# ScalarE makes the masked step sizes of a Mamba-2 layer as 32 scaled 128x128 copies per pair, in place of four products on GpSimd

## What is computed

```
dt = jax.nn.softplus(dt + dt_bias)
A = -jnp.exp(A_log)
dA = jnp.exp(dt * A)

def step(h, inp):
    dA_t, dtx_t, B_t, C_t = inp
    h = h * dA_t[:, :, None, None] + dtx_t[..., None] * B_t[:, None, None, :]
    y = jnp.einsum('bhpn,bn->bhp', h, C_t)
    return (h, y)
```

## Time and profile before

| | us |
|---|---|
| median of three runs | 860.14 |
| lowest and highest of them | 856.6, 867.21 |
| span of the profiled execution, first to last instruction | 851.0 |

### The profile page before, as it was taken

One profiled execution on the slowest core, in us unless ns is written; L12 is line 12 of the kernel. 1 busy time (PEld: TensorE's weight loads), 2 busy tenths in 40 slices (PEclk: granted clock), 3 DMA queues, 4 the chain that ended last, 5 costly groups with the idle time before them and its releaser, 6 DMA issues. The chain is left out here.

```text
span 851.0 us, 13516 instructions
## 1 busy us (share of the span) xinstructions
PE 689.8 (81%) x3713; PEld 528.2 (62%) x3713; DVE 608.2 (71%) x1640; ACT 447.5 (53%) x967; POOL 543.4 (64%) x398
## 2 busy tenths in 40 slices
PE   3687897788788899979998999799993865577883
PEld 3255665567467677857786778567882744355662
DVE  2839969988987998999879987998673364122331
ACT  3665666565675677648755776376532321121230
POOL 1414333746547587867867788678678587537775
PEclk9798799798798999989989999899997798697997
DMA  5000001112114544554465345534755677757882
GB/s 185 12 1 0 1 26 38 50 51 63 44 49 123 137 117 95 135 129 111 95 162 117 91 112 113 145 69 112 175 132 126 169 174 163 169 130 149 202 180 26
DMA packets 81273, 88.85 MB, mean 104 GB/s; under 512 B 7360, under 2 KB 67696, under 8 KB 81200
## 3 DMA queue, kind: packets, MB, share of 16 engines
q1 hardware_dynamic: 54528, 61.37, 25.4%
q0 software_dynamic: 26672, 26.62, 17.4%
HBM read 54.50 MB, written 33.46 MB: 103 GB/s over the span
## 5 line engine op out<-in xcount | busy, mean ns | idle before, releaser
L466 POOL DMA_INDIRECT out<-xs x142 | 228.7, 1611 | 115.4 <-issue 53.3
L436 POOL DMA_INDIRECT rows<-payload,pos x128 | 133.3, 1041 | 46.4 <-issue 30.9
L884 DVE SCALAR_TENSOR_TENSOR xbc<-T,table,xbc 128x511 f32<-128x511 f32 (+2 forms) x192 | 141.7, 746 | 7.6 <-ACT xbc L616 3.0
L1459 PE MATMUL FX<-wt,hid 128*128 128x128 f32 x568 | 89.7, 305 | 19.6 <-DVE hid L1129 19.5
L658 ACT ACTIVATE sg<-FG,wt 128x256 f32<-128x256 f32 x142 | 59.3, 470 | 83.2 <-PE FG L1446 83.1
L1137 DVE SCALAR_TENSOR_TENSOR xs<-FX,xs 128x128 f32<-128x128 f32 x142 | 43.0, 344 | 80.7 <-PE FX L1459 80.7
L1459 PEld LDWEIGHTS FX<-wt,hid 128*128 128x128 f32 x568 | 75.3, 207 | 29.7 <-DVE hid L1129 22.5
L1446 PE MATMUL FV<-xt,wt 128*128 128x256 f32 x284 | 81.7, 414 | 12.6 <-DVE hid L1129 12.4
L1129 DVE SCALAR_TENSOR_TENSOR hid<-FV,wt,sg 128x256 f32<-128x256 f32 x142 | 61.9, 477 | 41.8 <-ACT sg L658 26.2
L665 ACT ACTIVATE xt<-FX 128x256 f32<-128x256 f32 x71 | 27.2, 382 | 116.2 <-PE FX L1436 114.4
L1446 PE MATMUL FG<-xt,wt 128*128 128x256 f32 x284 | 78.7, 402 | 6.6 <-DMA wt<-in_wt 6.0
(11 more groups left out here) (207 smaller groups left out, 1397.8 us busy)
## 6 DMA issues: line engine op xcount, KB each, us to landing
wt<-in_wt SPq DMA_DIRECT2D x71, 386.0 KB, 4.4
xs<-rows SPq DMA_DIRECT2D x71, 258.0 KB, 3.6
x<-in_x SPq DMA_DIRECT2D x8, 512.0 KB, 3.8
out<-x SPq DMA_DIRECT2D x8, 512.0 KB, 3.7
out<-xs POOLq DMA_INDIRECT x142, 4.1
rows<-pad SPq DMA_DIRECT2D x8, 258.0 KB, 4.1
rows<-payload,pos POOLq DMA_INDIRECT x128
gate_a<-gates SPq DMA_DIRECT2D x8, 128.0 KB, 4.2
```

The costliest lines, as they stand in the source:

```text
L436: pool.indirect_dma_start(d["rows"], bass.IndirectOffsetOnAxis(ap=pos[:, k, n:n + 1], axis=0), payload[:, n, :], None).then_inc(scattered, 16)
L466: pool.indirect_dma_start(d["out"], bass.IndirectOffsetOnAxis(ap=xs[:, t % XSR, c, PAY - 1:PAY].bitcast(U32), axis=0), xs[:, t % XSR, c, 0 ...
L884: last = nc.vector.scalar_tensor_tensor(out=xbc[:, t, k, tap:L], in0=T[:, k, 0:L - tap], scalar=w, in1=xbc[:, t, k, tap:L], op0=ALU.mult, ...
L1459: last = nc.tensor.matmul(FX[:, TR + c * D:TR + (c + 1) * D], hid[:, t % 2, f, c * P:(c + 1) * P], wt[:, t % WR, DOWN + f * D:DOWN + (f + ...
```

## The change

`masked_da` goes from the POOL queue to the ACT queue. It waits for the same two semaphores and raises `mda_ready` once a chunk, as before. In place of one product of 128x1024 it issues 8 `Copy` activations of 128x128, each of which reads `upto` and takes one column of `da` as its scale: 32 a pair. The four calls of an iteration stand behind `z_silu(i + 1, 0)`, behind `conv_silu(i + 1, 2)`, behind `z_silu(i + 1, 1)` and behind `z_silu(i + 1, 2)`. Nothing else moves.

```
-            def masked_da(f, c):
-                pool.wait_ge(da_ready, f + 1)
-                wait(pool, seg_psum, J * (f - 1) + 2 * c + 2)
-                nc.gpsimd.tensor_tensor(out=mda[:, c, :, :], in0=upto[:, :].unsqueeze(1).to_broadcast([P, 2 * NH, P]),
-                                        in1=wide(da[:, c * J:(c + 1) * J], P), op=ALU.mult).then_inc(mda_ready, 1)
...
+            def masked_da(f, c):
+                act.wait_ge(da_ready, f + 1)
+                wait(act, seg_psum, J * (f - 1) + 2 * c + 2)
+                for n in range(J):
+                    last = nc.scalar.activation(mda[:, c, n, :], upto, ACT.Copy, scale=da[:, c * J + n:c * J + n + 1])
+                last.then_inc(mda_ready, 1)
...
                 if is_pair(i + 1):
                     z_silu(i + 1, 0)
+                    masked_da(i + 1, 0)
...
                     conv_silu(i + 1, 2)
+                    masked_da(i + 1, 1)
...
                     z_silu(i + 1, 1)
+                    masked_da(i + 1, 2)
...
                     z_silu(i + 1, 2)
+                    masked_da(i + 1, 3)
```

More of the change, by code:

```diff
@@ L490, in _ @@
                     add_out(PT * i - 24)
-                if is_pair(i + 1):
-                    masked_da(i + 1, 0)
-                    masked_da(i + 1, 1)
                 if is_pair(i - 1):
@@ L501, in _ @@
                     scatter(i - 1, 3)
-                if is_pair(i + 1):
-                    masked_da(i + 1, 2)
                 if is_tile(PT * i - 22):
                     add_out(PT * i - 22)
-                if is_pair(i + 1):
-                    masked_da(i + 1, 3)
                 if is_pair(i - 1):
```

## The result

The changed kernel takes 890.47 us (median of 4 runs, 888.65 to 894.05), beside 863.67 for the kernel before in the same comparison: a ratio of 1.0339, with a 95% interval of 1.0268 to 1.0411. On the 860.14 of before that is +29.2 us (+23.1 to +35.3), so 889; 891 was forecast. The profiled execution spans 886.8 us.

A forecast was written before the change was run, and what follows sets the result against it. DVE and PE bound the pairs' part before; ACT, from first `zs` to end of `h`, would bound it after. Growth of 52.0 less 21.2 of early stall gives 30.8; 860.1 + 30.8 = 891 us, range 866 to 914.

The forecast's parts named there:

- The bound: From first `zs` to end of `h`, ACT becomes the bound; this stretch grows 52.0 us over eight pairs; chance 0.70.
- the sum: Per pair, 9.4 us of copies less ACT's idle time less DVE's early stall; together 52.0 - 21.2 = 30.8 us.
- The pitch: Copies on ACT follow each other every 0.293 us, taken from four overlapping `xskip`; 9.4 us a pair, 74.9 in all.
- What was used up: ACT's idle time between first `zs` and end of `h`, 22.9 us over the pairs, is filled by copies to the last.
- one of the signs that I had named for a wrong forecast: The forecast is wrong if ACT still waits for PE or DVE between the copies.
- The return: DVE's early stall at `row_of` and `wtop` behind POOL's products goes and counts in full: 21.2 us over the pairs.
- The late standstill: DVE's stall at `ysum`, 11.2 us in all, gives nothing back; rival that it counts: 871 to 880 us, chance 0.18.
- The clock: PE's clock may fall before `project_out`, 917 us, chance 0.07, or rise elsewhere, 882 us; neither was taken into the forecast.
- the 26 us of that rival: `project_out` at half PE clock in seven pairs, 7 x 3.7 = 26 us more, 917; chance 0.07.
- the rise: With the early stall gone PE waits less before some stretches and clocks higher: at most 8.5 us gained, hence 882.
- Faster: Rival: copies fit into ACT's idle time before `h`, only the stalls count, 32.4 us gained, 828 us; chance 0.05.
- the offset of 9.1 us: The runs' median of 860.14 lies 9.1 us above the profiled span of 851.0; left as it is in the forecast.

The follow-up runs named there:

- The kernel with both kinds of work: Changed kernel with POOL's four products put back at their old places ahead of ACT's copies, which write the same values again: 908.35 us, ratio 1.0593.
- the kernel with all four moved: Kernel before, mask products still on POOL, first two behind two scatters and the fourth behind a later scatter; no copy on ACT: 838.31 us, ratio 0.9762.

## Why the prediction was right

**The bound.** The argument rested on ACT's 2 to 3.4 us of idle time between the first `zs` and the end of `h`, not on its 53%. That stretch grew by 6.5, 6.5, 7.4, 7.4, 5.8, 5.4, 5.8 and (to the first decay) 5.9 us over the eight pairs: 50.8, for 52.0 in the sum. The pitch is the 0.293 of the earlier trace rows. With 0.41 us a copy, which is the budget of the Trainium skill ("ScalarE: Activation LUTs", "Rules for kernel authors"), the sum was about 920; the trace disagrees, since one copy takes 399 ns by itself but eight in a row take 2.34 us.

**What was used up.** ACT still waits 0.15 us in pair 4, 0.65 in pair 1; the sum had zero, and taken strictly this is one of the signs that I had named for a wrong forecast. It is small beside the 3.4 and 3.1 that it had. That the waits on DVE, on the projection and on the last taps would go was right.

**The return.** What the pairs give back outside the stretch, from the shift of the first decay: 0.8, 0.5, 2.4, 4.5, 0.8, 4.6, 3.5, 4.1, which is 21.1 for 21.2 in the sum. The total is as near as this partly by luck. Pair by pair the net was 5.7, 6.0, 5.1, 2.9, 5.0, 0.8, 2.4, 1.8, for a forecast of 7.0, 4.4, 4.7, 4.7, 3.5, 1.2, 3.5, 1.9: single terms are off by up to 1.8 us, both ways, and sum to 29.7 for 30.8. Pair 3 shows a term that the sum had left out. From the first decay of pair 2 to the first `zs` of pair 3, in the kernel before and in the changed one (columns of the earlier trace rows):

```profile
179.66:234.25 54.59, 45.01 (x234) 34.79 (x232) 48.65 (x142) 32.17 (x67) 31.29 (x25) 0.84 0.18 58
196.41:246.49 50.08, 41.98 (x234) 31.85 (x232) 43.28 (x130) 32.17 (x67) 25.48 (x21) 0.90 0.18 59
```

The standstill there is 2.5 us, and 4.5 came back. PE did the same 234 matmuls in 3.0 us less, at a granted clock of 0.90 in place of 0.84. The kernel without a mask has 0.90 there too, and also gives back 4.5; the one with the standstill put back has 0.84, and gives back nothing. The one with half the copies lies between: 3.4 came back at 0.83, so the clock is not all of the surplus. Ahead of pair 2, where the clock is 0.90 before and after, 2.4 came back for 2.5. So the products on POOL cost a standstill and, as far as these rows go, some of PE's clock behind it. In other pairs less came back than the sum had (0.8 for 2.5 in pair 4), and the two errors met. No run separates the clock's part of the 21.1 from the standstill's.

**The late standstill.** The sum let it count for nothing and gave 0.18 to its counting. The kernel with both kinds of work shows, by the length of the stretches (49.7 and 50.8), that it does count for nothing as long as ACT bounds them; the one without a mask shows that half of it would come back if ACT did not.

**The clock.** I said that PE's clock might fall ahead of `project_out` or rise elsewhere, and took neither. Both happened. It rose between the stretches, as shown for pair 3: from 0.84 to 0.90 there, and from 0.91, 0.95, 0.92 and 0.95 to 1.00, 0.97, 1.00 and 0.97 ahead of pairs 4 to 7. And it fell in the stretch, to 0.79 in pair 0 and 0.83 or 0.84 in pairs 1 to 6 where it was 1.00. In pair 4 the place is the front of it:

```profile
327.98 3.44 PE L1346 MATMUL YA<-xdt,decay 128*128 128x64 f32 x16 [3.08 <-ACT zs L615]
```

```profile
327.98:333.00 5.02, 5.02 (x18) 4.02 (x19) 3.45 (x6) 5.02 (x20) 2.00 (x2) 0.53 0.31 66
```

That is the same work as the one from 313.65 in 1.89 us at full speed, behind a wait of 3.08 us, at a granted clock of 0.53. It costs little or nothing, since ACT, which bounds the stretch, idles for only 0.15 us of it. `project_out` itself runs at 3.81 us, as before (3.74), and in no pair at more than 3.99, so the 26 us of that rival did not come. I had the fall, and looked for it at the wrong end of the stretch; the rise I had priced at 8.5 us and then left out of the sum.

**Faster.** The Trainium skill's rule on the ports ("SBUF — State Buffer", "Who interferes with whom") names the mechanism. The traces agree that VectorE stands still beside GpSimd's product and ScalarE does not (in the kernel before, `xskip` takes its 0.39 us beside a product as elsewhere), and that taking the products away gave back 21 us, the clock's part included; that a lock on ports is the cause no run shows. The rule prices one side only. The move was slower by as much as ACT's place cost more than that.

**Where the numbers were off.** ACT's busy time rose by 71.7, not by about 100: busy time does not count the overlap twice (256 copies make 78.2, while 256 x 399 ns would be 102), and I read the mean as if it added up. And the offset of 9.1 us that I carried from span to median was not what it looked like. In every other profiled execution of the study the run's time is 1.7 to 1.9 us above its span. What made the span of before short is its tail: from the first decay of pair 7 to the end it has 277.2 us, where the changed kernel has 283.3 and the eight experiments 282.4 to 284.8. The difference of the two spans, 35.8, is 29.7 from the pairs and 6.1 from that tail, in which nothing was changed. Carrying the offset was right, for a reason that I had not seen. What made that one tail shorter is open.

## What to carry to other kernels

Before work is moved to the engine with the lowest share, take the stretch in which it will stand, and subtract that engine's idle time there from what is added: 9.4 us into 2.2 to 3.4 cost more than the whole gain (53 us against the kernel without a mask from pair 1 on), and the same copies placed elsewhere in the same queue cost 14. When the reason for moving is a standstill of DVE behind GpSimd, look first at whether the GpSimd work can be moved in its own queue to where DVE runs something else; a few calls in another order gave 20 us here (13 to 28), where moving it to another engine lost 29. A stall whose removal frees an engine is worth something only if nothing else is late at the point where that engine is next waited for, and whether that is so can change with the very edit that removes it.

## What the runs showed of the hardware

- DVE's standstill does not hang on its own size: `wtop`, 128x8 and 0.17 us by itself, took up to 4.98 us. It goes where the product goes: `ysum`, `y` and `wo` each stood still in one version or another, for 2.85 us, 1.58 us and 1.40 us (the row at 391.03) over the length that they have alone.
- Not every DVE instruction beside a product stands still. In the kernel with all four moved, three of one size run beside two products. The two that read a PSUM bank (YB, YA) take their usual 0.68 and 0.69 us, and the one that reads `ysum` and `xskip`, neither of which is in PSUM, takes 1.95, until half a microsecond behind the second product's end:

```profile
159.20 3.77 POOL L426 TENSOR_TENSOR mda<-table,da 128x1024 f32<-128x1024 f32 x2
160.13 0.68 DVE L944 TENSOR_TENSOR ysum<-YB,edge 128x512 f32<-128x512 f32 x1
160.85 0.69 DVE L948 TENSOR_TENSOR ysum<-YA,ysum 128x512 f32<-128x512 f32 x1
161.57 1.95 DVE L950 TENSOR_TENSOR ysum<-ysum,xskip 128x512 f32<-128x512 f32 x1
```

  The taps, which read `T` in PSUM, keep their 0.75 us beside a product as well. What else stands still beside GpSimd can be read in a trace in the same way before its work is placed.
- PE at half clock behind waits of 2.0 and 3.1 us on ACT, in the rows above, in stretches that ran at 1.00 before.
- Waits that I can't explain. In pair 4 of the changed kernel ACT and DVE wait together for results in `S` and in YA and YB, whose matmuls end by 316.0 in PE's timeline:

```profile
320.15 0.60 ACT L592 ACTIVATE yt<-S 128x512 f32<-128x512 f32 x1 [2.99 <-remote]
```

```profile
320.09 0.69 DVE L942 TENSOR_TENSOR ysum<-YB,edge 128x512 f32<-128x512 f32 x1 [2.46 <-remote]
```

  The trace calls the releaser remote. Such waits stand in the changed kernel and in all eight experiments, none in the trace of before. They may be why pair 4 gave back 0.8 us in place of 2.5; no run was made to find their cause.
